# Three layer norms read from PSUM, the residual added there by TensorE, and each batch's result signalled on its own

## The reference, cut to what matters

```python
def _layernorm(x, axis=-1, eps=1e-05):
    m = jnp.mean(x, axis=axis, keepdims=True)
    v = jnp.var(x, axis=axis, keepdims=True)
    return (x - m) / jnp.sqrt(v + eps)
...
    x = _layernorm(x + _L0_attn_ref(x, ...), axis=-1)     # norm 0
    x = _layernorm(x + _L0_xattn_ref(x, ctx_768, ...), axis=-1)   # norm 1
    x = _layernorm(x + _L0_ffn_ref(x, ...), axis=-1)      # norm 2
    x = _layernorm(x + _L1_attn_ref(x, ...), axis=-1)     # norm 3
    x = _layernorm(x + _L1_xattn_ref(x, ctx_768, ...), axis=-1)   # norm 4
    x = _layernorm(x + _L1_ffn_ref(x, ...), axis=-1)      # norm 5
```

## Time and profile before

| | |
|---|---|
| median of three runs | 524.66 us (519.0 to 525.67) |
| the profiled execution | 521.54 us, its span 519.4 us |
| mean granted PE clock over the span | 0.956 |
| busy share of the span | PE 89%, DVE 53%, ACT 44%, POOL 21% |

### The profile page before, as it was taken

One profiled execution on the slowest core, in us unless ns is written; L12 is line 12 of the kernel. 1 busy time (PEld: TensorE's weight loads), 2 busy tenths in 40 slices (PEclk: granted clock), 3 DMA queues, 4 the chain that ended last, 5 costly groups with the idle time before them and its releaser, 6 DMA issues.

```text
span 519.4 us, 10977 instructions
## 1 busy us (share of the span) xinstructions
PE 464.5 (89%) x4144; PEld 333.6 (64%) x4144; DVE 277.2 (53%) x698; ACT 230.6 (44%) x419; POOL 107.8 (21%) x227
## 2 busy tenths in 40 slices
PE   8698989988589998899999598998898999999993
PEld 3265767765346984356667466877786677777773
DVE  4735768715781537554524688888334333333326
ACT  3834757750222414224564246766604543333440
POOL 4202435423200102212112242342200000000001
PEclk9699999998959999989999789999999999999997
DMA  6866455150400001553111000100000011111111
GB/s 178 321 181 146 135 140 150 42 190 6 163 0 1 1 1 42 158 153 107 37 30 40 11 15 14 52 1 1 1 2 11 22 41 41 41 31 29 41 32 41
DMA packets 23307, 34.40 MB, mean 66 GB/s; under 512 B 7600, under 2 KB 16000, under 8 KB 23008
## 3 DMA queue, kind: packets, MB, share of 16 engines
q1 hardware_dynamic: 23264, 33.81, 22.2%
HBM read 28.26 MB, written 5.24 MB: 64 GB/s over the span
## 4 chain that ended last, share of the span: by engine, by line
PE 61%; issue 14%; DVE 9%; DMA 6%; POOL 5%; ACT 4%; SPq 1%; POOLq 0%; DVEq 0%; ACTq 0%
PE ps L1044 11%; PE ps L1027 11%; POOL probs L576 4%; PE ps L643 4%; PE ps L621 4%; PE ps L608 3%; PE ps L597 3%; DMA arena<-mT 3%; PE ps L1015 3%; PE ps L850 2%; ACT arena L1092 2%; PE ps L884 2%; PE ps L655 2%; DVE bst L1411 2%; PE ps L605 2%
## 5 line engine op out<-in xcount | busy, mean ns | idle before, releaser
L1368 DVE TENSOR_REDUCE negm<-ps 128x4 f32<-128x512 f32 x96 | 64.0, 688 | 38.2 <-PE ps L608 37.1
L1683 DVE SCALAR_TENSOR_TENSOR racc<-ps,sm,racc 128x128 f32<-128x128 f32 x128 | 35.9, 344 | 63.2 <-PE ps L1044 63.1
L1092 ACT ACTIVATE arena<-ps,w1a 128x512 f32<-128x512 f32 x64 | 43.4, 687 | 59.0 <-PE ps L1027 57.8
L1092 ACT ACTIVATE probs<-ps 128x512 f32<-128x512 f32 (+1 forms) x100 | 56.4, 592 | 25.4 <-PE ps L621 24.4
L1044 PEld LDWEIGHTS ps<-w1a,arena 128*128 128x128 f32 x512 | 59.4, 192 | 7.2 <-issue 6.2
L1044 PE MATMUL ps<-w1a,arena 128*128 128x128 f32 x512 | 59.8, 275 | 0.8 <-DVE racc L1674 0.8
L1027 PE MATMUL ps<-xT,w1a 128*128 128x512 f32 x128 | 57.9, 594 | 1.4 <-ACT xT L1092 1.4
L1092 ACT ACTIVATE arena<-ps 128x512 f32<-128x512 f32 (+4 forms) x71 | 39.7, 581 | 36.2 <-PE ps L850 15.9
L597 PE MATMUL ps<-onesb 128*128 128x512 bf16 x134 | 38.8, 418 | 3.0 <-DVE sm L1546 2.1
L576 POOL TENSOR_TENSOR probs<-probs,rzE 128x480 f32<-128x480 f32 x32 | 30.6, 986 | 52.0 <-DVE rzE L1625 52.0
L532 POOL TENSOR_SCALAR rstd<-mv 128x4 f32<-128x4 f32 x12 | 2.7, 226 | 184.6 <-DVE mv L1414 184.6
(11 more groups left out here) (210 smaller groups left out, 806.9 us busy)
## 6 DMA issues: line engine op xcount, KB each, us to landing
stackA<-arena SPq DMA_DIRECT2D x12, 256.0 KB, 3.3
arena<-stackA SPq DMA_DIRECT2D x24, 96.0 KB
arena<-stackA SPq DMA_DIRECT2D x8, 288.0 KB
w1a<-in_w1a SPq DMA_DIRECT2D x1, 2048.0 KB, 8.9
w2a<-in_w2a SPq DMA_DIRECT2D x1, 2048.0 KB, 7.6
w1a<-in_w1b SPq DMA_DIRECT2D x16, 128.0 KB, 2.0
w1a<-in_w2b SPq DMA_DIRECT2D x16, 128.0 KB, 2.0
stackD<-arena SPq DMA_DIRECT2D x6, 256.0 KB
```

The lines of the kernel that those rows point to most:

```text
L1092: return nc.scalar.activation(o, i, f, **kw)
L1368: nc.vector.tensor_reduce(negm[:, slot % 2, 4 * g:4 * g + 4], tiles(bank(BANK_S + g % 2), 4, P), AX.X, ALU.max, negate=True).then_inc(a.ma ...
L1683: last = stt(racc[:, b, :], bank(banks + half)[:, k * P:(k + 1) * P], sm[:, 11, bass.ds(b * E1 + e, 1)], racc[:, b, :], ALU.mult, ALU.add)
```

## The change

At norms 0, 3 and 4 a new function `residual` multiplies the identity by a half of `xres` (one float32 product, 128 x 512) with start=True, which lays x in the bank that the output projection then adds to (start=False). `sums_at` says which banks: M0 and O at norm 0, O and T + 1 at norm 3, M0 and M1 at norm 4; `summed(k, b)` gives batch b's sum there, or `racc` for the other norms. DVE's three pairs of adds are gone, and `ln_stats` and `ln_apply` read the bank. The five `keep_busy` products of `finish` are gone; two residual products stand in their place before norm 0, one before norm 3, whose second stands between the halves of L719. Norm 4's first residual product stands in the last `pair_step` before the fourth group of weight transposes, behind a wait for POOL's bias and for ACT's last copies out of BANK_M0; its second is ahead of L1015. At all six norms `ln_apply` signals `ln_out` for each batch, and `to_feature_half` waits for each batch before its transpose. The transposes of norms 0 and 4 go to other banks (S and O).

```diff
+        sums_at = {0: (BANK_M0, BANK_O), 3: (BANK_O, BANK_T + 1), 4: (BANK_M0, BANK_M1)}
+        def summed(k, b):
+            return bank(sums_at[k][b // 4])[:, b % 4 * P:(b % 4 + 1) * P] if k in sums_at else racc[:, b, :]
...
+            def residual(k, half):
+                mm(bank(sums_at[k][half]), ident, half_of(xres, half).rearrange("p b n -> p (b n)"), start=True, stop=True)
-            def finish(a, chunks, w):
-                keep_busy(5, BANK_T)
+            def finish(a, norm, chunks, w):
+                residual(norm, 0)
+                if chunks == 2:
+                    residual(norm, 1)
                 pe.wait_ge(a.norm, NH if chunks == 2 else PAIRS)
...
                 for half in range(2):
                     pe.wait_ge(a.postc, (half + 1) * B // per // 2)
-                    for k in range(4):
-                        b = 4 * half + k
+                    if chunks == 1 and half == 1:
+                        residual(norm, 1)
+                    for b in range(4 * half, 4 * half + 4):
                         for c in range(chunks):
-                            last = mm(bank(BANK_O + half)[:, k * P:(k + 1) * P], oT[:, b, c, :],
-                                      w[:, c, :] if chunks == 2 else w[:],
-                                      start=c == 0, stop=c == chunks - 1)
+                            last = mm(summed(norm, b), oT[:, b, c, :], w[:, c, :] if chunks == 2 else w[:],
+                                      start=False, stop=c == chunks - 1, skip_group_check=True)
...
             def to_feature_half(k, half, at=BANK_M0):
-                pe.wait_ge(ln_out, 2 * k + half + 1)
                 for j in range(4):
+                    pe.wait_ge(ln_out, B * k + 4 * half + j + 1)
                     last = nc.tensor.transpose(bank(at + half)[:, j * P:(j + 1) * P], xres[:, 4 * half + j, :], ident)
...
                 pair_weights(n, slot, 2)
+                if n == PAIRS - 1:
+                    pe.wait_ge(e_vc, 2 * PAIRS)
+                    pe.wait_ge(resb, 3)
+                    residual(4, 0)
                 pair_weights(n, slot, 3)
...
+            residual(4, 1)
             pe.wait_ge(e_oc, 2 * PAIRS)
...
             def ln_stats(k, half):
-                    dch(nc.vector.bn_stats(bst[:, b, :], racc[:, b, :]))
+                    dch(nc.vector.bn_stats(bst[:, b, :], summed(k, b)))
...
             def ln_apply(k, half):
-                    last = ts(xres[:, b, :], racc[:, b, :], mv[:, b, 0:1], rstd[:, b:b + 1], ALU.subtract, ALU.mult)
-                    if b < s[-1]:
-                        dch(last)
-                last.then_inc(ln_out, 1)
+                    ts(xres[:, b, :], summed(k, b), mv[:, b, 0:1], rstd[:, b:b + 1], ALU.subtract, ALU.mult
+                       ).then_inc(ln_out, 1)
...
-                link(tt(half_of(racc, half), tiles(bank(BANK_O + half), 4, P), half_of(xres, half), ALU.add))
                 ln_stats(0, half)
```

More of the change, by code:

```diff
@@ L448, in _ @@
             for half in range(2):
-                sp.wait_ge(ln_out, 2 * 5 + half + 1)
+                sp.wait_ge(ln_out, B * 5 + 4 * half + 4)
                 sp.dma_start(out[:, 4 * half:4 * half + 4, :], xres[:, 4 * half:4 * half + 4, :]).then_inc(g_out, 16)
@@ L538, in add_bias @@
                 pool.wait_ge(ln_xT, 2 * k)
-                pool.wait_ge(ln_out, 2 * k)
+                pool.wait_ge(ln_out, B * k)
                 nc.gpsimd.tensor_tensor(xres[:], xres[:], over(bias[:], B), ALU.add).then_inc(resb, 1)
@@ L715, in finish, with to_feature @@
                     pe.wait_ge(a.postc, (half + 1) * B // per // 2)
-                    for k in range(4):
-                        b = 4 * half + k
+                    if chunks == 1 and half == 1:
+                        residual(norm, 1)
+                    for b in range(4 * half, 4 * half + 4):
                         for c in range(chunks):
-                            last = mm(bank(BANK_O + half)[:, k * P:(k + 1) * P], oT[:, b, c, :],
-                                      w[:, c, :] if chunks == 2 else w[:],
-                                      start=c == 0, stop=c == chunks - 1)
+                            last = mm(summed(norm, b), oT[:, b, c, :], w[:, c, :] if chunks == 2 else w[:],
+                                      start=False, stop=c == chunks - 1, skip_group_check=True)
                     last.then_inc(a.y, 1)
             def to_feature_half(k, half, at=BANK_M0):
-                pe.wait_ge(ln_out, 2 * k + half + 1)
                 for j in range(4):
+                    pe.wait_ge(ln_out, B * k + 4 * half + j + 1)
                     last = nc.tensor.transpose(bank(at + half)[:, j * P:(j + 1) * P], xres[:, 4 * half + j, :], ident)
                 last.then_inc(ln_tp, 1)
-            def to_feature(k):
+            def to_feature(k, at=BANK_M0):
                 for half in range(2):
-                    to_feature_half(k, half)
+                    to_feature_half(k, half, at)
             def project_keys(n):
@@ L798, in _ @@
             heads(A, NH, pair=False, causal=False)
-            finish(A, 2, wproj0)
+            pe.wait_ge(ld_l, 16 * 6)
+            finish(A, 0, 2, wproj0)
             keep_busy(10, BANK_T)
-            to_feature(0)
+            to_feature(0, BANK_S)
             for half in range(2):
@@ L911, in _ @@
             heads(D, PAIRS, pair=True, causal=True)
-            finish(D, 1, woD)
+            pe.wait_ge(resb, 2)
+            finish(D, 3, 1, woD)
             def project_queries(n):
@@ L1011, in _ @@
             for half in range(2):
-                for k in range(4):
-                    b = 4 * half + k
+                for b in range(4 * half, 4 * half + 4):
                     for p in range(PAIRS):
-                        last = mm(bank(BANK_O + half)[:, k * P:(k + 1) * P], otall[:, p, b * P:(b + 1) * P], woE[:, p, :],
-                                  start=p == 0, stop=p == PAIRS - 1)
+                        last = mm(summed(4, b), otall[:, p, b * P:(b + 1) * P], woE[:, p, :],
+                                  start=False, stop=p == PAIRS - 1, skip_group_check=True)
                 last.then_inc(e_y, 1)
@@ L1050, in _ @@
             for half in range(2):
-                to_feature_half(4, half)
+                to_feature_half(4, half, BANK_O)
                 pe.wait_ge(ln_xT, 8 + half + 1)
@@ L1151, in feature_copy, with feature_copies @@
                 fn(xT[:, half * HALF:(half + 1) * HALF], bank(at + half), ACT.Copy).then_inc(ln_xT, 1)
-            def feature_copies(k):
+            def feature_copies(k, at=BANK_M0):
                 for half in range(2):
-                    feature_copy(k, half)
+                    feature_copy(k, half, at)
             def table_of(f):
@@ L1193, in _ @@
             finish(A, 2)
-            feature_copies(0)
+            feature_copies(0, BANK_S)
             for half in range(2):
@@ L1205, in _ @@
             for half in range(2):
-                act.wait_ge(ln_out, 2 + half + 1)
+                act.wait_ge(ln_out, B + 4 * half + 4)
                 fn(half_of(xpart[:, 0], half), half_of(xres, half), ACT.Copy).then_inc(f_hi, 1)
@@ L1323, in _ @@
             table_of(ACT.Gelu)
-            feature_copies(4)
+            feature_copies(4, BANK_O)
             def gelus(e, slot, first=False):
@@ L1501, in _ @@
             ln_apply(1, 1)
-            dve.wait_ge(ln_out, 4)
+            dve.wait_ge(ln_out, 2 * B)
             for half in range(2):
```

## The result

| | before | changed |
|---|---|---|
| median of 16 runs each | 520.87 us | 518.11 us |
| lowest of 16 | 518.77 us | 514.86 us |
| ratio of the changed kernel to before | | 0.9926, 95% interval 0.9899 to 0.9953 |
| the profiled execution, its span | 521.54, 519.4 us | 518.67, 516.6 us |
| mean granted PE clock | 0.956 | 0.955 |

It says 3.9 us quicker (2.4 to 5.3), the medians 2.8, the two profiles 2.9. The page of the changed kernel reads much like that of before; DVE's share of the chain fell from 9% to 6%.

What follows compares the result with a forecast made beforehand. PE carried 61% of the chain, DVE 9%, so stages were judged singly: 1.0 + 0.5 + 0.3 - 0.1 + 0.15 = 1.85 us, 3.45 with the clock. From 523.1 that gave 519.7 us, range 515.6 to 524.8.

Steps and rivals of the forecast that it cites:

- Norm 0: First norm's stage, from its product to the next projection: 1.0 us shorter, without the clock.
- the two terms: At norm 0: half 1's statistics 0.81 us earlier, less 0.15 for reading PSUM; transposes signalled by batch save 0.3.
- The cover on PE: At norm 0: residual products cost PE 0.53 us more than fillers, hidden in its 0.74 us wait for POOL.
- Reading PSUM: DVE's statistics 12 ns and applying 25 ns slower per instruction from PSUM, 0.15 us on a norm's path.
- The clock after norm 0: Next projection after norm 0: a shorter PE gap keeps the clock up, 1.6 us saved; least certain, 0 or 1.6.
- Rival A: After norm 0 the clock is halved all the same, or nothing can be given back: 521.2 us, chance 0.27.
- sign of being wrong: Anywhere in the changed profile: a window with the clock at 0.50 where before had none.
- Norms 1 and 2: Only signals change there; transposes run under DVE's applying: 0.5 us saved at norm 1, 0.3 at norm 2.
- Norm 3: PE bounds it; second residual product delays L938, mostly covered by a wait: loss of 0.1 us.
- Norm 4: Residual products delay L1015 by 0.8 us, but the add goes and transposes run earlier: gain of 0.15 us.
- B: After norm 2 the clock is halved too, L896 at half rate, up to 3.5 us: 524.8 us, chance 0.10.
- C: At norms 0, 3 and 4 PSUM reads eat the gain, 0.46 us each: 522.5 us without the clock, chance 0.13.

Runs made afterwards that it cites:

- two opposite edits: Four PE fillers added after norm 0 to the kernel before: ratio 0.9992; the ten fillers after norm 0's product removed from the changed kernel: ratio 0.9956.
- kernel with norm 0 only: Changed kernel with its signals, but the residual product at norm 0 alone, norms 3 and 4 back to adds on DVE: 516.39 us, ratio 0.992.

## Why the prediction was right, point by point

The measured 518.11 us lies in the range of 515.6 to 524.8, and the gain by the ratio, 3.9 us, stands beside the forecast 3.45. The stages account for 2.2 to 2.3 us of it without the clock, forecast at 1.85, and the signals alone are worth nearly all of that; what makes up the rest is not settled (see the clock below). The base was off more than the change: I took 523.1 us for the kernel before, and 16 runs put it at 520.87.

**Norm 0** was forecast at 1.0 us and the stage measures 0.9. Signals alone give 0.3 of it and the residual products 0.5, which were the two terms (0.3 and 0.81 less the reading). The cover on PE held, by a little: two residual products in 1.88 us where five fillers took 1.24, and L724 starts at once behind POOL, with no wait left for PE where 0.74 us was the earlier trace rows. The last transpose ends 0.4 us after the last applying (124.35 in the chain; L1443 ends at 122.61 + 1.36), as forecast, for the four now run batch by batch from 123.07.

```profile
112.15 1.88 PE L710 MATMUL ps<-xres,con 128*128 128x512 f32 x4
...
114.13 1.97 PE L724 MATMUL ps<-con,oall 128*128 128x128 f32 x16
...
122.61 1.36 DVE L1443 TENSOR_SCALAR xres<-ps,mv,rstd 128x128 f32<-128x128 f32 x4 [0.21 <-POOL rstd L540]
...
123.07 1.28 PE L741 MATMUL ps<-con,xres 128*128 128x128 f32 x4 [0.29 <-DVE xres L1443]
```

**Reading PSUM** is the term that was mis-sized. I took 25 ns for an applying instruction, near the row of the same width, L1683. That row reads two tensors, one of them in SBUF, and has no partner with both in SBUF, so its 344 ns held no price of PSUM. The measured 62 lies near the 67 that the pair of one-source rows gave. For statistics I took 12 and it is 5. Four of each make 0.27 us in place of 0.15. The rule of the Trainium skill in "VectorE: DVE Perf Modes", section "Why PSUM operands drop a tier", described this case: the trace agrees, 400 against 338 ns. The 65 ns more for each instruction, my estimate from the same page's errata section, would give nearly the same for applying. It does not hold for the statistics, which show 5, nor for a two-tensor add of 512 columns, at 691 ns with one input in PSUM (L1688) and 692 with both in SBUF (L1522). Nor could it give the 538 ns of the 1024-column pair.

**The clock after norm 0** was forecast at 1.6 us, with doubt. It held in both profiles of the changed kernel and fell in both of the kernel before; the stage to the first maxima gives 1.5 and the next one 0.3. The two opposite edits show that PE's gap decides it in the profile. Rival A, that it is halved all the same, is out for these executions, and its gain of 1.85 us lies below the ratio's interval, which starts at 2.4. But the stretch is not always gone from the profile. Eight profiles are of kernels with the changed kernel's code at norm 0. In all eight the first projection ran at full clock, and in two of them a halved stretch stood one stage later, at 129 to 133 and at 131 to 136, and took 0.7 and 1.1 us back.

Over the whole span of the profiles nothing was gained in clock, 0.956 against 0.955. The changed kernel's first profile had another such stretch at 43 to 47 us, in front of anything the change touches:

```profile
44.00:45.00 1.00, 1.00 (x4) 0.29 (x2) 0.00 (x0) 0.00 (x0) 0.00 (x0) 0.50 0.76 156
```

By the prediction's own words this is a sign of being wrong, a window at 0.50 where before had none. The second profile of the kernel before has a stretch there too (42 to 47), so the change did not bring it. The mean clock of all executions in the ratios says the same as the two spans: 0.957 for the changed kernel over 13, 0.957 for the kernel before over the 76 beside the experiments, where one stretch less would make 0.003. So 1.8 us is the value of this place in a profile, and an average gain in clock is not shown. That the measured 3.9 us lies so near the forecast 3.45, of which 1.6 was this term, is in part luck: the stages without the clock make 2.2 to 2.3, and what the other 1.6 are is open.

**Norms 1 and 2** were forecast at 0.5 and 0.3, and measure 0.6 to 0.7 and 0.3 to 0.4. The chain of the changed kernel still has norm 1's transposes in half clock, 1.24 us.

**Norm 3** was forecast at a loss of 0.1 and came at 0 to 0.1, but out of two parts of which I had one. The late second half of PE's work I had: the residual products cost 0.3 to 0.4 us against the adds. What I left out is that the signals let the transposes run as the batches come, in the 0.55 us in which PE waited, and that gives 0.4 by itself. Both together cancel, and the transposes stand right behind L953 with no wait, as said:

```profile
270.15 1.02 PE L710 MATMUL ps<-xres,con 128*128 128x512 f32 x2
...
272.33 1.16 PE L733 MATMUL ps<-woD,oT 128*128 128x128 f32 x8 [0.25 <-ACT oT L1111]
...
273.32 1.02 PE L710 MATMUL ps<-xres,con 128*128 128x512 f32 x2
...
275.08 3.79 PE L953 MATMUL ps<-arena,ctxT 96*120 96x128 f32 x32
...
278.71 0.60 PE L741 MATMUL ps<-con,xres 128*128 128x128 f32 x4
```

**Norm 4** was forecast at 0.15 and gave 0.3: from the third group of weight transposes to the next projection it is 366.13 to 389.05 = 22.9 us, and was 368.65 to 391.91 = 23.3. The cost in front of the product was over-sized. The fourth group starts 0.4 us late and not 0.6 (367.49 where 367.08 would be the old distance of 0.95 from the third), and L1034 another 0.15 behind it, where I had 0.2. The residual product takes 0.86 us in the chain, near the 0.89 that I took, but its records begin at 366.62, before those of the third group end at 366.78, and the fourth group's begin at 367.49, before its own end at 367.64. The transposes start right behind the ten fillers, as worked out.

```profile
366.13 0.65 PE L977 MATMUL ps<-con,probs 128*120 128x128 f32 x4 [0.29 <-POOL probs L582]
...
366.62 1.02 PE L710 MATMUL ps<-xres,con 128*128 128x512 f32 x2
...
367.49 0.60 PE L977 MATMUL ps<-con,probs 128*120 128x128 f32 x4
...
369.91 1.12 PE L710 MATMUL ps<-xres,con 128*128 128x512 f32 x2
...
370.88 14.45 PE L1034 MATMUL ps<-oT,arena 128*128 128x128 f32 x128
...
385.17 2.32 PE L603 MATMUL ps<-onesb 128*128 128x512 bf16 x10
...
387.32 0.98 PE L741 MATMUL ps<-con,xres 128*128 128x128 f32 x4
...
389.05 1.98 PE L1046 MATMUL ps<-xT,w1a 128*128 128x512 f32 x4 [0.75 <-ACT xT L1111]
```

The gain of 0.3 is not the sum's, though. The kernel with signals alone, all adds on DVE, takes the same 22.9 us from the third group to the next projection, and the kernel without signals 23.3, as before. At norm 4 the signals give all, and moving the add gives nothing. The kernel before:

```profile
368.65 0.65 PE L962 MATMUL ps<-con,probs 128*120 128x128 f32 x4 [0.29 <-POOL probs L576]
...
391.91 1.98 PE L1027 MATMUL ps<-xT,w1a 128*128 128x512 f32 x4 [0.75 <-ACT xT L1092]
```

Signals alone:

```profile
366.51 0.65 PE L984 MATMUL ps<-con,probs 128*120 128x128 f32 x4 [0.29 <-POOL probs L582]
...
389.45 1.98 PE L1048 MATMUL ps<-xT,w1a 128*128 128x512 f32 x4 [0.75 <-ACT xT L1113]
```

**The rivals.** B, a halved clock after norm 2, came in no profile of the study. C, reads from PSUM that eat the gain, took 91 ns more for applying and 24 for the statistics; they measured 62 and 5, and 0.27 us for a norm does not eat the 0.8 of norm 0.

## What to carry to other kernels

Signal each part of a result that another engine can start on. It cost no instruction that the page counts, and with the adds left in place it gave 2.2 us of the stages. Moving the adds on top of that gave 0.6 at norm 0 (8.8 to 8.2 us), nothing at norm 4 and lost 0.4 at norm 3. So moving a sum into the matmul's bank pays where PE waits in front of the product and DVE is on the path behind it (norm 0); where PE has its own work up to the transposes (norm 3) it costs time. And before a gain is put down to the clock, take a second profile of the same kernel to see which stretch belongs to the place, and compare the mean clock of many executions.

## What was not expected of the hardware

A one-source fp32 instruction of 128 columns with two pointer scalars loses 62 ns when its source is in PSUM, the statistics instruction of the same width 5 ns. A halved stretch of the clock that a shorter gap removes can come back one stage later: 125 to 129 us before, 129 to 133 with signals alone and in the kernel with norm 0 only, none there in the changed kernel's two profiles. And every kernel in which norm 4's half 0 was applied early, five profiles of four kernels, had one stretch of 3.4 us between 389 and 412 us that the kernel before and the changed kernel did not have in their two profiles each (the kernel without signals had one at 411); six fillers in the stage ahead did not remove it, and the cause was left open.
